# Attention scores over all rows of a zero-padded query tile, and value matmuls gathered by sets of four heads

## What is computed

```python
q = (xn @ q_w + q_b).reshape(B, L, H, hd)      # H = 16, hd = 8, L = 512
k = (xn @ k_w + k_b).reshape(B, L, H, hd)
v = (xn @ v_w + v_b).reshape(B, L, H, hd)
scores = jnp.einsum('bqhd,bkhd->bhqk', q, k) * hd ** (-0.5)
scores = jnp.where(causal[None, None], scores, -jnp.inf)
attn = jax.nn.softmax(scores, axis=-1)
attn_out = jnp.einsum('bhqk,bkhd->bqhd', attn, v).reshape(B, L, Dm) @ o_w + o_b
...
_, ys = jax.lax.scan(step, h0, (x_c..., dt..., Bm..., Cm...))   # h = exp(dt A) h + dt x B;  y = C h
x = x + alpha * attn_out + (1.0 - alpha) * ssm_out
```

## Time and profile before

| | |
|---|---|
| median of 3 runs | 2010.07 us (1996.1 to 2011.77) |
| the profiled execution | 2013.56 us |
| its span, first to last instruction | 2011.8 us |
| share of the span: PE, DVE, ACT, POOL | 88%, 68%, 54%, 42% |
| mean granted TensorE clock | 0.893 |

### The profile page before, as it was taken

The page is one execution under the profiler, slowest core; times in us unless marked ns, Lnnn a source line. Parts: engine busy times, 40 slices in busy tenths (PEclk is TensorE's granted clock), DMA queues, the critical chain, the costliest instruction groups (busy, mean ns, idle before and its releaser), DMA issues. The chain is left out here.

```text
span 2011.8 us, 21952 instructions
## 1 busy us (share of the span) xinstructions
PE 1766.1 (88%) x7090; PEld 939.2 (47%) x7090; DVE 1374.8 (68%) x2071; ACT 1078.6 (54%) x1784; POOL 845.6 (42%) x863
## 2 busy tenths in 40 slices
PE   4868989989989899899899987898999999988778
PEld 3333333333333333333333324555877777763573
DVE  1595767756767767667677705857776767756876
ACT  3734545453454455444454446646878787852107
POOL 1363536644555455345365433121222222216762
PEclk9965989987989899778898998988999999987889
DMA  2221101110111121011111002100111111100001
GB/s 75 69 61 56 58 22 58 53 57 34 56 56 43 39 62 53 25 55 53 36 57 46 17 1 84 49 22 24 37 48 43 47 38 48 39 20 0 0 1 42
DMA packets 61679, 84.74 MB, mean 42 GB/s; under 512 B 6600, under 2 KB 32062, under 8 KB 61566
## 3 DMA queue, kind: packets, MB, share of 16 engines
q1 hardware_dynamic: 61466, 83.31, 13.6%
q10 hardware_dynamic: 100, 0.03, 0.0%
HBM read 74.38 MB, written 8.78 MB: 41 GB/s over the span
## 5 line engine op out<-in xcount | busy, mean ns | idle before, releaser
L988 PE MATMUL bank<-PT,Vb 128*32 128x512 f32 (+3 forms) x1024 | 339.1, 481 | 12.7 <-ACT Os L1507 12.7
L1677 POOL TENSOR_TENSOR dBx<-dtx,Bb 128x512 f32<-128x512 f32 x256 | 319.9, 1272 | 15.8 <-DMA Bb<-b_dram 9.2
L1548 ACT ACTIVATE bank<-dtv,alog 128x512 f32<-128x512 f32 x256 | 176.3, 690 | 279.1 <-DVE hst L1257 278.2
L1290 DVE TENSOR_TENSOR hl<-lsq,hh 128x512 fp32r<-128x512 f32 x320 | 248.1, 783 | 97.6 <-ACT hh L1564 91.1
L1237 DVE TENSOR_REDUCE Mx<-bank 128x1 f32<-128x384 f32 (+3 forms) x352 | 217.6, 630 | 134.6 <-PE bank L988 134.3
L988 PE MATMUL bank<-QK 48*128 48x128 bf16 (+7 forms) x1024 | 275.1, 328 | 34.1 <-DVE Mx L1237 28.5
L1257 DVE TENSOR_TENSOR_SCAN hst<-bank,dBx 128x512 f32<-128x512 f32 x256 | 297.9, 1204 | 4.3 <-POOL dBx L1677 4.3
L1657 POOL TENSOR_SCALAR_AFFINE_SELECT PT<-PT 128x256 f32<-128x256 f32 (+1 forms) x320 | 118.2, 372 | 433.2 <-ACT PT L1504 432.2
L1561 ACT ACTIVATE lsq<-bank,vcol 128x512 f32<-128x512 f32 x320 | 220.3, 693 | 112.0 <-DVE hl L1290 63.3
L1504 ACT ACTIVATE PT<-bank 128x512 f32<-128x512 f32 x320 | 186.1, 590 | 171.5 <-PE bank L988 170.3
L1175 DVE SCALAR_TENSOR_TENSOR yT<-bank,bc,yT 128x256 f32<-128x256 f32 x480 | 200.4, 476 | 101.6 <-PE bank L1091 101.5
(11 more groups left out here) (247 smaller groups left out, 2532.9 us busy)
## 6 DMA issues: line engine op xcount, KB each, us to landing
Bb<-b_dram SPq DMA_DIRECT2D x128, 256.0 KB, 3.4
stage<-w_rows SPq DMA_DIRECT2D x64, 256.0 KB, 3.2
parts<-part SPq DMA_DIRECT2D x16, 384.0 KB, 2.8
QK<-parts SPq DMA_DIRECT2D x64, 96.0 KB
QK<-parts SPq DMA_DIRECT2D x64, 64.0 KB
stage<-in_L_ffn_We_dram SPq DMA_DIRECT2D x16, 256.0 KB, 3.4
hst<-in_L_attn_x_dram SPq DMA_DIRECT2D x8, 256.0 KB, 5.6
QK<-parts SPq DMA_DIRECT2D x64, 32.0 KB
```

The lines of the kernel that those rows point to most:

```text
L988: return engine.matmul(o, l, r, start=start, stop=stop, tile_position=pos, skip_group_check=True)
L1290: engine.tensor_tensor(hl[:, sl, :], full[:, f, :], hh[:, sl, :].bitcast(F32), ALU.subtract).then_inc(sems["dve_hl"], 1)
L1548: engine.activation(bank[4 + h][:], dtv[:, b % 2, h, :], ACT.Exp, scale=alog[:, h, n:n + 1]).then_inc(sems["act_da"], 1)
L1677: engine.tensor_tensor(dBx[:, sl, h], dtx[:, b % 2, h], Bb[:, sl], ALU.mult).then_inc(sems["pool_dbx"], 1)
```

## The change

Four things are changed.

1. `QK` gets three slabs: 0 holds the queries of head `h = 0` on rows 0 to 47 with zeros elsewhere, 1 the queries of head `h = 1` on rows 64 to 111 with zeros elsewhere, and 2 the keys of both heads. The one/maximum row moves to row 127. Every score matmul now contracts over all rows (127 for `max`, 128 for `att`), and the zero rows of the queries blank out the other head. GpSimd zeroes the three slabs at the start, and SyncE waits for that before it writes the row of ones.
2. `weigh` is gathered: one step for each set (four heads with 512 columns; four with 384 and 128; four with 256), its matmuls sorted by key block and then by head, so that four neighbours write four different strips of 32 partitions. A set is weighed when the next set's last `att` step has been issued.
3. `PT` has 10 slots instead of 6.
4. To make room, `mrow` and `dtr` share a tile and `gtmp` lies in `On`.

The number of matmuls, their columns, the exponentials, the selects, the maxima and the transfers stay as they were, but for one transfer of ones less.

```diff
-NPT = 6
-LAG = 4
+NPT = 10
-    def weigh(b, g, parts, sl, x, y):
+    def weigh(b, g, units):
         k = 3
-        it = step("weigh", b=b, g=g, parts=parts, sl=sl, bank=k, free=free.get(f"b{k}"), ready=(x, y, r_v[b]))
-        it["m"] = free[f"PT{sl}"] = up("pe_av")
+        it = step("weigh", b=b, g=g, bank=k, free=free.get(f"b{k}"), ready=(r_v[b], [(x, y) for _, _, x, y in units]),
+                  blocks=sorted((kj, i, off, sl) for parts, sl, _, _ in units for i, kj, off in parts))
+        it["m"] = up("pe_av")
+        for _, sl, _, _ in units:
+            free[f"PT{sl}"] = it["m"]
         return it["m"]
...
-            units = [[(i, 0, 0)] for i in range(4)] + [[(i, 1, 0), (i, 3, 384)] for i in range(4)] + \
-                [[(i, 2, 0), (i + 2, 2, 256)] for i in range(2)]
-            for parts in units:
+            sets = [[(i, 0, 0)] for i in range(4)], [[(i, 1, 0), (i, 3, 384)] for i in range(4)], [[(i, 2, 0), (i + 2, 2, 256)] for i in range(2)]
+            for parts_of in sets:
...
+                    if len(units) == len(parts_of):
+                        late.append((b, g, units, parts_of is sets[2]))
+                    settle(1)
...
-            QK = tmp("QK", [P, 2, 3, 4, T], BF16)
+            QK = tmp("QK", [P, 3, 3, 4, T], BF16)
...
-                        mm(o[:, kc * i:kc * i + kc], QK[64 * h:64 * h + 48, 0, s, a, P * qi:P * qi + P], QK[64 * h:64 * h + 48, 1, s, a, 0:kc],
+                        mm(o[:, kc * i:kc * i + kc], QK[0:127, h, s, a, P * qi:P * qi + P], QK[0:127, 2, s, a, 0:kc],
...
-                        x = mm(o[:, off:off + n], QK[64 * h:64 * h + 49, 1, s, a, P * kj:P * kj + P], QK[64 * h:64 * h + 49, 0, s, a, P * kj:T])
+                        x = mm(o[:, off:off + n], QK[:, 2, s, a, P * kj:P * kj + P], QK[:, h, s, a, P * kj:T])
...
-                    for i, kj, off in it["parts"]:
+                    for kj, i, off, sl in it["blocks"]:
...
+            for j in range(3):
+                engine.memset(QK[:, j].rearrange("p s a t -> p (s a t)").bitcast(F32), 0.0).then_inc(sems["pool_set"], 1)
...
-            for h in range(2):
-                engine.dma_start(QK[64 * h + 48:64 * h + 49, 1], mrow[0:1, 0:1, :].broadcast_to([1, 12, T])).then_inc(sems["ld_one"], 16)
+            q.wait_ge(("pool_set", pool_set["qz2"]))
+            engine.dma_start(QK[127:128, 2], mrow[0:1, 0:1, :].broadcast_to([1, 12, T])).then_inc(sems["ld_one"], 16)
```

More of the change, by code:

```diff
@@ L227, in settle @@
         while len(late) > n:
-            b, g, parts, sl, x, y, end = late.pop(0)
-            m = weigh(b, g, parts, sl, x, y)
+            b, g, units, end = late.pop(0)
+            m = weigh(b, g, units)
             if end:
@@ L241, in attend @@
             g = 2 * hf + gg
-            units = [[(i, 0, 0)] for i in range(4)] + [[(i, 1, 0), (i, 3, 384)] for i in range(4)] + \
-                [[(i, 2, 0), (i + 2, 2, 256)] for i in range(2)]
-            for parts in units:
[L245 to L256, removed]
+            sets = [[(i, 0, 0)] for i in range(4)], [[(i, 1, 0), (i, 3, 384)] for i in range(4)], [[(i, 2, 0), (i + 2, 2, 256)] for i in range(2)]
+            for parts_of in sets:
+                units = []
+                for parts in parts_of:
+                    k = take()
+                    sl = pts[0] % NPT
+                    pts[0] += 1
+                    it = step("att", u=u, gg=gg, parts=parts, sl=sl, bank=k, free=free.get(f"b{k}"), ready=(r_mr[u], r_qk[u]),
+                              pt_free=free.get(f"PT{sl}"))
+                    it["m"] = up("pe_sc")
+                    it["x"] = free[f"b{k}"] = up("act_exp")
+                    it["y"] = up("pool_sel")
+                    m = it["m"]
+                    units.append((parts, sl, it["x"], it["y"]))
+                    if len(units) == len(parts_of):
+                        late.append((b, g, units, parts_of is sets[2]))
+                    settle(1)
+                    yield
         free[f"QK{s}"] = m
@@ L939, in on_set @@
             return {name: i + 1 for i, name in enumerate(names.split())}
-        pool_set = on_set("vrow qk0 qk1 qk2 qk3 wo id0 id om cm on ep mask0 mask idb sel0 sel bsum vb0 mr vb")
+        pool_set = on_set("vrow qk0 qk1 qk2 qk3 wo id0 id om cm on ep mask0 mask idb sel0 sel bsum vb0 mr vb qz0 qz1 qz2")
         dve_set = on_set("row0 row1 sc0 sc1 neg abs sgn2 max sgn gate om1 av2 av3 A qbs")
@@ L1056, in tensor_program @@
                         x = mm(o[32 * i:32 * i + 32, P * kj:T], Vb[:, b % 2, kj, 36 * g + 9 * i:36 * g + 9 * i + 32],
-                               PT[:, it["sl"], off:off + n], start=(kj == 0), stop=(kj == 3), pos=(0, 32 * i))
+                               PT[:, sl, off:off + n], start=(kj == 0), stop=(kj == 3), pos=(0, 32 * i))
                     x.then_inc(sems["pe_av"], 1)
@@ L1757, in sync_program @@
                                 x = src[h, k:k + 1].broadcast_to([n, 8, 4 * T]) if i == 0 else src[h, 0:n]
[L1758 removed]
+                                engine.dma_start(QK[64 * h + 8 * r:64 * h + 8 * (r + n), h if i == 0 else 2, s].rearrange("p a t -> p (a t)"),
                                                  x).then_inc(sems[f"qk_in{s}"], 16)
@@ L1763, in sync_program @@
                     for h in range(2):
-                        engine.dma_start(QK[64 * h + 48:64 * h + 49, 0, s], mrow[4 * h:4 * h + 4, s2, :]).then_inc(sems[f"mrow_in{s2}"], 16)
+                        engine.dma_start(QK[127:128, h, s], mrow[4 * h:4 * h + 4, s2, :]).then_inc(sems[f"mrow_in{s2}"], 16)
                 elif kind == "dbc":
```

16 lines of the change are left out of this document (9 added, 7 removed).

## The result

The changed kernel takes 1903.73 us (median of 4 runs, 1897.98 to 1907.24) against 2010.92 us of the kernel before: a ratio of 0.946, with a 95% interval of 0.939 to 0.954. So it is faster by 107 us, where 235 had been forecast, and outside the stated range (1735 to 1865).

What follows compares the result with a forecast made beforehand. TensorE was taken to bound the attention rounds, VectorE after the change. Rounds of 1021.6 us were to become 737 + 34 + 17, with 3 saved at the start: 2013.6 - 237 = 1777, then 1775; range 1735 to 1865.

Steps and rivals of the forecast that it cites:

- TensorE sets the time before the change: First fourteen attention rounds: TensorE is the bound, busy 860.0 of 942.8 us, 91%, against VectorE's 72%.
- Value matmuls in sets: Attention rounds: four strips overlap, so value matmuls take 4.3 instead of 15.4 us, freeing 11.1 us of TensorE a round.
- full rows: Score matmuls over 127 or 128 rows remove 80 shape changes of 0.105 us, 8.4 us of TensorE a round.
- the rival without overlap: Neighbouring strips run one after another, TensorE keeps its 15.4 us of value matmuls a round; time 1874, chance 0.07.
- VectorE becomes the bound: Fourteen rounds: TensorE falls below VectorE's 43.3 (light) and 54.5 us (heavy); with 2.5 us of waits, light rounds take 45.8.
- a sign of being wrong: In the profile after: VectorE at 80% with waits for Mx as long as before would show the prediction wrong.
- Heavy rounds, 61.6 us: Six rounds with the next batch's entry: 54.5 us of VectorE plus 7.1 of chain waits, down from 77.2.
- VectorE can be kept full: Interleaving does not starve VectorE: from 102 to 133 us, without value matmuls, it is busy 30.9 of 31.0 us.
- The last two rounds: Rounds 14 and 15: 34 us instead of 50.8, and 17 instead of 28.0 with ScalarE's exponentials setting the pace.
- The start: Before 180 us: 8.4 us of memsets hidden in idle GpSimd time; first maxima lose 60 shape changes, gaining 3 us.
- VectorE's waits stay: In-order lists couple engines and half of VectorE's 268 us idle stays; time 1856, chance 0.18 shared with a clock near 0.75.
- The low clock: Idle TensorE drops to low clock; slower than before below a mean of 0.54; chance 0.05, shared with an unseen wait.

Runs made afterwards that it cites:

- e2: Changed kernel with padded score rows kept but gathering undone (six slots, lag of four, one weigh per unit): 1955.93 us, 0.980 of the kernel before.
- e4: Changed kernel with the two SiLU activations shrunk to a one-column copy and the table loads dropped, so output differs: 1862.66 us, 0.933 of the kernel before.
- e11: Kernel before the change, with SiLU activations shrunk to a one-column copy and table loads dropped: 1995.77 us, 1.001 of the kernel before.
- e7: Changed kernel with the gate's matmul ahead of the convolution and an empty step on either side of SiLU: 1883.63 us, 0.946 of the kernel before.
- e10: Changed kernel with e7's entry order and SiLU computed in pieces from already loaded functions, products on GpSimd: 1837.96 us, 0.924 of the kernel before.
- e1: Changed kernel with the padding undone (scores over 48 and 49 rows), gathered value matmuls kept: 2038.75 us, 1.022 of the kernel before.
- e9: Changed kernel plus one tiny 48-row matmul before each maximum and score unit, bringing shape changes back: 1915.09 us, 0.964 of the kernel before.
- e3: Changed kernel with each set's matmuls sorted by head, then key block: 1906.0 us, 0.955 of the kernel before.

## Why the prediction was wrong

**TensorE sets the time before the change: right.** The time fell with TensorE's work and e2, with 6 us of TensorE's busy time less in a light round (45.4 for 51.4), has light rounds of 52.1 for 55.7.

**Value matmuls in sets, 11.1 us a round; full rows, 8.4: right in size.** A set of four takes 0.99 us (about 1 expected), 3.9 times as fast as one by one, and the change of shape is gone. The neighbouring strips overlap four at a time, and the rival without overlap is out. In a light round TensorE is busy 36.9 us where 31.9 were forecast; by an estimate from the clocks (31.9 x 0.97 / 0.90 = 34.4), 0.90 instead of 0.97 explains half of that.

**VectorE becomes the bound: right in the light rounds only.** They take 49.0 us on average for 45.8, with VectorE busy 42 of 49.5, 84% and not 95. Its waits there fell from 12.9 to 7.6 us, and I had put 2.5. That is 24 us in all. A part of it may be the clock; this was not separated. Over the fourteen rounds VectorE is busy for 79%, close to the 80% that the prediction had named as a sign of being wrong; its waits for `Mx` did fall, from 129.2 us in the sixteen rounds to 73.1.

**Heavy rounds, 61.6 us: the step that failed.** "What stays are waits along a chain ... the entry of the next batch in a heavy one (3.2 and 0.9 us, and half of the 6.1 for transposes, 7.1 us)." I took the waits of the earlier trace rows as what the chain costs. They are what the chain showed beyond TensorE's backlog. The chain itself was longer and lay under the backlog: SiLU's block with its table loads (6.3 us a round by e4, nothing before the change by e11), the gate's matmul behind the convolution (4.6 us by e7), and with both the matmuls at 1.2 GHz that follow an idle TensorE. The wait that I named in the earlier trace rows, 3.9 us before 561, was the second of them; I used it for the clock and forgot it in the sum. With the block broken up and the gate's matmul moved, e10's heavy rounds take 393.9 us instead of 456.6: that is 63 of the 87 us by which they missed the forecast. What the other 24 are stays open. e2 shows the same from the other side: with TensorE's work down and its value matmuls still one by one, the heavy rounds hardly fell, and in the one shown VectorE's longest wait for the transposes is 7.1 us.

**VectorE can be kept full: a row that was true and told too little.** From 102 to 133 us no attention runs, so no score unit stands in TensorE's list in front of a transpose and waits for ScalarE. The row showed that two engines can be interleaved, not three. This is read from the plan; no run tried it.

**The last two rounds, 51 us for 62.2.** Round 15 came at 16.9 for 17. Round 14 took 45.3 for 34, with no engine over 32 us busy: another chain, which no run looked into. The start came 3 us later instead of 3 earlier; that was not followed up either.

**The rivals.** "VectorE's waits stay" is the one that came true in kind: waits in the fourteen rounds fell from 268 to 177 us, where it had half of them, 134, and it gave 1856; against the 1904 measured it, too, was short. "The low clock" was given 0.05 to turn the sign, together with waits not seen; in the changed kernel the clock stayed at 0.88. But it was nearer than that number says: e1, the change without its padding, is that rival, at a clock of 0.69 and slower than before. The reckoning that it decides at 0.54 holds for the changed kernel. For e1, which keeps the changes of shape (8.4 us a round, 134 in sixteen), the same reckoning gives (550 + 134) / 1021.6, a clock of 0.67, and e1 was next to that. I had costed the padding by the changes of shape alone (8.4 us a round), and e9 shows that these are worth some 10 us of the whole, at most 35, and the rest of the padding's gain goes with the clock.

## What to carry to other kernels

When a bounding engine gets faster, list the longest single piece of work on every other engine and ask who stands in line behind it: such a piece can be invisible as long as the bounding engine has a backlog, and the waits of the profile before need not contain it. Here it was a function table switched for two activations, two loads of 1.28 us around 2 us of work. The runs took this block away whole (e4) or broke it up (e10); the loads alone were not priced.

Overlapping small matmuls went with a lower clock here (0.88 to 0.69, and 0.95 to 0.88 with padding); try such a change by itself and look at the granted clock of the stretch before you count the gain. Zero rows, which cost no time by column, went with a higher one.

## What the hardware showed that I had not expected

The rows of a matmul went with the clock. Scores over 48 and over 127 or 128 rows take the same time by column, but with the gathered sets the granted clock of the fourteen rounds is 0.69 with the first and 0.88 with the second (0.89 in e9, where only the rows are left of the padding).

The order of a set's matmuls in the list did not matter for their overlap, in the one other order that was tried. In e3 the list goes head by head, 384 columns and then 128 of the same strip; the four 384-column matmuls start within 0.04 us all the same, and the set takes 1.0 us.

At full clock a matmul of another shape costs 0.105 us before it, 32 against 128 output columns or 48 against 128 rows. e9 has 42 such pairs more in a light round: 41.5 - 36.9 = 4.5 us of busy time, half of the 9 expected. From start to start its trace has nearly the whole: at 594.77 us 0.107 from the tiny matmul to the next, and at 595.11 us 0.312 for a mask matmul of 512 columns (0.213) ahead of a tiny one. The busy time shows less because the clock of that round is 0.93 instead of 0.90 and, as I take it, because a record reaches beyond the next start anyway (the tiny matmul's lasts 0.175 us), so that a part of the pause was counted as busy before.
